# One graph-network kernel on one core: the message stage scales gathered rows instead of masks

## What is computed

```
xg0 = y0[edge_src]                                   # (E, 64)
xg1 = y1[edge_src]                                   # (E, 64, 3)
mid0 = w_a * xg0 * ea0
mid1 = w_b * einsum('euc,ec->eu', xg1, ea1) / sqrt(3)
mid2 = (w_c * xg0)[:, :, None] * ea1[:, None, :]
mid3 = (w_d * ea0)[:, :, None] * xg1
mids = concatenate([mid0, mid1, mid2, mid3])         # (E, 8 * 64)
agg  = segment_sum(mids, edge_dst, num_segments=n)   # (n, 512)
```

## Time and profile before

| what | value |
|---|---|
| median of three timed runs | 2001.14 us (1994.2 to 2003.65) |
| span of the profiled execution, first to last instruction | 2413.3 us |
| mean granted clock of TensorE | 0.875 of full speed |
| busy in the span: PE, PEld, DVE, ACT, POOL | 1891.3, 1517.9, 1125.8, 1021.4, 1104.5 us |
| DMA | 376.43 MB, mean 156 GB/s |

### The profile page before, as it was taken

The page is one execution under the profiler, slowest core; times in us unless marked ns, Lnnn a source line. Parts: engine busy times, 40 slices in busy tenths (PEclk is TensorE's granted clock), DMA queues, the critical chain, the costliest instruction groups (busy, mean ns, idle before and its releaser), DMA issues. The chain is left out here.

```text
span 2413.3 us, 38460 instructions
## 1 busy us (share of the span) xinstructions
PE 1891.3 (78%) x9911; PEld 1517.9 (63%) x9911; DVE 1125.8 (47%) x2791; ACT 1021.4 (42%) x3052; POOL 1104.5 (46%) x1499
## 2 busy tenths in 40 slices
PE   1368787877799858999455877787778789899699
PEld 1245454554466657999335766676767679777588
DVE  3532222222242374544664666565656669431322
ACT  2513343343353532333264555454545557454222
POOL 5547667666700004555375665565655550000243
PEclk7679999889999858999777888887888889999799
DMA  5636556565734026666544554555554553255553
GB/s 150 202 90 198 190 187 198 185 193 187 210 140 138 11 64 201 212 212 215 135 149 147 150 159 140 151 155 145 147 153 144 150 148 107 69 164 177 155 180 129
DMA packets 229197, 376.43 MB, mean 156 GB/s; under 512 B 66081, under 2 KB 114308, under 8 KB 228998
## 3 DMA queue, kind: packets, MB, share of 16 engines
q1 hardware_dynamic: 174820, 222.13, 31.0%
q0 software_dynamic: 52224, 150.15, 20.2%
q10 hardware_dynamic: 1954, 1.79, 0.2%
HBM read 275.38 MB, written 99.57 MB: 155 GB/s over the span
## 5 line engine op out<-in xcount | busy, mean ns | idle before, releaser
L1940 POOL DMA_INDIRECT msg_got<-y_dram,block_src x416 | 412.4, 991 | 293.5 <-DVE msg_prod L2012 139.7
L439 POOL DMA_INDIRECT ffn_w<-xn_dram,block_src x384 | 364.6, 949 | 219.2 <-issue 81.7
L1961 ACT ACTIVATE msg_scaled<-msg_plain,msg_w 128x125 f32<-128x125 f32 x1044 | 314.0, 386 | 280.1 <-DVE msg_plain L1993 234.6
L554 PE MATMUL sum_ps_bank<-ffn_w,sum_onehot 128*125 x928 | 270.5, 419 | 115.6 <-DVE sum_onehot L893 84.3
L554 PEld LDWEIGHTS sum_ps_bank<-ffn_w,sum_onehot 128*125 128x125 f32 x928 | 184.0, 206 | 264.6 <-issue 246.6
L881 DVE TENSOR_TENSOR agg<-sum_ps_bank,agg 125x256 f32 x232 | 98.4, 424 | 432.4 <-PE sum_ps_bank L554 216.5
L541 PE MATMUL sum_ps_bank<-sum_fc,sum_space 128*128 128x512 f32 x416 | 231.9, 644 | 68.9 <-ACT sum_space L639 48.3
L650 ACT ACTIVATE sum_space<-sum_ps_bank,sum_rec 128x128 f32<-128x128 f32 x416 | 131.0, 369 | 330.4 <-PE sum_ps_bank L541 159.5
L1982 PE MATMUL msg_ps_z<-msg_prod,msg_scaled 128*125 128x128 f32 x1416 | 207.5, 293 | 53.7 <-issue 53.0
L1982 PEld LDWEIGHTS msg_ps_z<-msg_prod,msg_scaled 128*125 128x125 f32 x1416 | 198.6, 206 | 72.4 <-issue 64.1
L2022 DVE TENSOR_TENSOR agg<-msg_ps_z,agg 125x512 f32 x232 | 159.4, 687 | 23.9 <-issue 5.2
(11 more groups left out here) (343 smaller groups left out, 3397.9 us busy)
## 6 DMA issues: line engine op xcount, KB each, us to landing
edge_w<-sum_space SPq DMA_DIRECT2D x52, 1040.0 KB
msg_w<-edge_w SPq DMA_DIRECT2D x174, 260.0 KB
ffn_run_w<-in_L_ffn_w SPq DMA_DIRECT2D x64, 512.0 KB
x_sb<-edge_w SPq DMA_DIRECT2D x58, 260.0 KB
ffn_rows<-agg SPq DMA_DIRECT2D x25, 448.0 KB
ffn_w<-in_L_ffn_w SPq DMA_DIRECT2D x16, 512.0 KB, 8.7
wd<-in_L_ffn_Wd SPq DMA_DIRECT2D x8, 1024.0 KB, 8.6
msg_got<-y_dram,block_src POOLq DMA_INDIRECT x416
```

The lines of the kernel that those rows point to most:

```text
L439: pool.indirect_dma_start(got[:, (b + 1) % RING, u, :], None, k.x if b < RAW else k.xn_dram, bass.IndirectOffsetOnAxis(ap=k.block_src[:, b ...
L554: last = pe.matmul(ps_sum[n % ZB][0:P, :], onehot[n % OB][:, u, :], got[:, ds(need % RING, 1), u, :].rearrange("p o d -> p (o d)"), start= ...
L1940: pool.indirect_dma_start(got[:, (b + 1) % RING, u, :, :].rearrange("p k v -> p (k v)"), None, k.y_dram, bass.IndirectOffsetOnAxis(ap=k.bl ...
L1961: last = act.activation(scaled[s % MB][:, x, c, :], plain[s % MB][:, c, :], ACT.Copy, scale=w[s % RS][:, c, D + x:D + x + 1])
```

## The change

ScalarE scales gathered rows instead of masks. For each column of 128 edges and each component x of the edge vector it multiplies two planes of the gathered row, plane 0 and plane x + 1, by that component, into a new buffer `turned` (two halves: plane 0 times each component, and plane x + 1 times component x). It reads the gathered rows by a register, and so waits for `blocks_in` and no longer for the mask. VectorE then forms all eight planes complete: it adds the three products of the second half to the dot product (two instructions, in a buffer `dots`), and multiplies planes 0 and 1 to 3 as before, planes 5 to 7 from the first half of `turned`, and plane 4 from `dots`. TensorE sums all eight planes under the plain mask, with one matmul of 512 columns for each column of edges. `scaled` is gone, `turned` has three buffers, and SyncE no longer waits for ScalarE.

```diff
@@ -1887,10 +1887,10 @@
 
         w = [borrow(CH * WREC).rearrange("p (c d) -> p c d", c=CH) if b == 1 else ph.sb(f"w{b}", [128, CH, WREC])
              for b in range(RS)]
-        plain = [borrow(CH * P).rearrange("p (c w) -> p c w", c=CH) if b == 1 else ph.sb(f"plain{b}", [128, CH, P])
-                 for b in range(MB)]
-        scaled = [borrow(3 * CH * P).rearrange("p (x c w) -> p x c w", x=3, c=CH) if b == 1 else ph.sb(f"scaled{b}", [128, 3, CH, P])
-                  for b in range(MB)]
+        plain = [ph.sb(f"plain{b}", [128, CH, P]) for b in range(MB)]
+        turned = [borrow(CH * 6 * MUL).rearrange("p (j c x v) -> p j c x v", j=2, c=CH, x=3) if b == 2
+                  else ph.sb(f"turned{b}", [128, 2, CH, 3, MUL]) for b in range(MB - 1)]
+        dots = [ph.sb(f"dots{b}", [128, CH, MUL]) for b in range(2)]
         prod = [borrow(CH * 8 * MUL).rearrange("p (c k v) -> p c k v", c=CH, k=8) if b == 2 else ph.sb(f"prod{b}", [128, CH, 8, MUL])
                 for b in range(XB)]
         ph.taken.append(k.x_put)
@@ -1898,8 +1898,8 @@
         ps_lanes, lanes_made, rest_zero = ph.ps("lanes", [128, P]), ph.sem("lanes_made"), ph.sem("rest_zero")
         w_in, got_in, blocks_in = ph.sems("w_in", RS), ph.sems("got_in", RING), ph.sem("blocks_in")
         rest, rested = ph.sb("rest", [128, 32]), ph.sem("rested")
-        masked, scaled_made, made, summed, added = (
-            ph.sem(x) for x in ("masked", "scaled_made", "made", "summed", "added"))
+        masked, scaled_made, made, summed, added, dotted = (
+            ph.sem(x) for x in ("masked", "scaled_made", "made", "summed", "added", "dotted"))
         block = ph.ctx.enter_context(nc.Block())
 
         @block.sync
@@ -1907,7 +1907,6 @@
             for s in range(NST):
                 if s >= RS:
                     sp.wait_ge(made, s - RS + 1)
-                    sp.wait_ge(scaled_made, s - RS + 1)
                 if s == 1:
                     sp.wait_ge(k.x_put, 32 * (NG - 1))
                 for h in range(2):
@@ -1951,36 +1950,45 @@
         def _(act):
             rest = k.agg[:, T // 2:T, :].rearrange("p t d -> p (t d)")
             act.activation(rest, k.ident[:, 0:1].to_broadcast([128, (T - T // 2) * 2 * D]), ACT.Copy, scale=0.0).then_inc(rest_zero, 1)
+
+            def place(n):
+                return act.value_load(k.pair_need[0:1, n:n + 1], min_val=1, max_val=NB)
+
+            need = [place(0), place(1)]
             for s in range(NST):
-                act.wait_ge(masked, s + 1)
+                if s == 1:
+                    act.wait_ge(k.x_put, 32 * (NG - 1))
                 act.wait_ge(w_in[s % RS], 32 * (s // RS + 1))
-                if s >= MB:
-                    act.wait_ge(summed, s - MB + 1)
-                for c in range(CH):
-                    for x in range(3):
-                        last = act.activation(scaled[s % MB][:, x, c, :], plain[s % MB][:, c, :], ACT.Copy,
-                                              scale=w[s % RS][:, c, D + x:D + x + 1])
+                act.wait_ge(blocks_in, need[1])
+                if s >= MB - 1:
+                    act.wait_ge(made, s - MB + 2)
+                following = []
+                for h in range(2):
+                    for u in range(KC):
+                        c = KC * h + u
+                        for x in range(3):
+                            last = act.activation(
+                                turned[s % (MB - 1)][:, :, c, x, :],
+                                got[:, ds(need[h] % RING, 1), u, 0:x + 2:x + 1, :].rearrange("p o k v -> p (o k) v"),
+                                ACT.Copy, scale=w[s % RS][:, c, D + x:D + x + 1])
+                    if s + 1 < NST:
+                        following.append(place(2 * s + 2 + h))
                 last.then_inc(scaled_made, 1)
+                need = following
 
         @block.tensor
         def _(pe):
             pe.matmul(ps_lanes[:, :], k.onesf[0:1, :], k.iota[0:1, 0:P], start=True, stop=True).then_inc(lanes_made, 1)
             for s in range(NST):
-                pe.wait_ge(scaled_made, s + 1)
+                pe.wait_ge(masked, s + 1)
                 pe.wait_ge(made, s + 1)
                 if s >= ZB // 2:
                     pe.wait_ge(added, 1 + 2 * (s - ZB // 2 + 1))
-                mask, by, p = plain[s % MB], scaled[s % MB], prod[s % XB]
+                mask, p = plain[s % MB], prod[s % XB]
                 for h in range(2):
-                    z = ps_z[(2 * s + h) % ZB]
                     for u in range(KC):
                         c = KC * h + u
-                        pe.matmul(z[0:P, 0:4, :], mask[:, c, :], p[:, c, 0:4, :], start=(u == 0), stop=False, skip_group_check=True)
-                    for x in range(3):
-                        for u in range(KC):
-                            c = KC * h + u
-                            last = pe.matmul(z[0:P, 4:6 + x:1 + x, :], by[:, x, c, :], p[:, c, 4 + x:8:3 - x, :],
-                                             start=False, stop=(x == 2 and u == KC - 1), skip_group_check=True)
+                        last = pe.matmul(ps_z[(2 * s + h) % ZB][0:P, :, :], mask[:, c, :], p[:, c, :, :], start=(u == 0), stop=(u == KC - 1))
                 last.then_inc(summed, 1)
 
         @block.vector
@@ -2000,18 +2008,25 @@
             def products(s, need):
                 p = prod[s % XB]
                 v = w[s % RS][:, :, 0:D].rearrange("p c (k v) -> p c k v", v=MUL)
+                from_0, from_1 = (turned[s % (MB - 1)][:, j, :, :, :] for j in range(2))
+                dot = dots[s % 2][:, :, :]
                 dve.wait_ge(w_in[s % RS], 32 * (s // RS + 1))
                 dve.wait_ge(blocks_in, need[1])
                 if s >= XB:
                     dve.wait_ge(summed, s - XB + 1)
+                dve.wait_ge(scaled_made, s + 1)
+                dve.tensor_tensor(dot, from_1[:, :, 0, :], from_1[:, :, 1, :], ALU.add).then_inc(dotted, 1)
                 for h in range(2):
                     y = got[:, ds(need[h] % RING, 1), :, :, :].rearrange("p o u k v -> p (o u) k v")
                     at = slice(KC * h, KC * h + KC)
-                    dve.tensor_tensor(p[:, at, 0:8:7, :], v[:, at, 0:4:3, :], y[:, :, 0:1, :].to_broadcast([128, KC, 2, MUL]), ALU.mult)
-                    for q in (1, 2):
-                        last = dve.tensor_tensor(p[:, at, 3 * q - 2:3 * q + 1, :], v[:, at, q:q + 1, :].to_broadcast([128, KC, 3, MUL]),
-                                                 y[:, :, 1:4, :], ALU.mult)
-                last.then_inc(made, 1)
+                    dve.tensor_tensor(p[:, at, 0, :], v[:, at, 0, :], y[:, :, 0, :], ALU.mult)
+                    dve.tensor_tensor(p[:, at, 1:4, :], v[:, at, 1:2, :].to_broadcast([128, KC, 3, MUL]), y[:, :, 1:4, :], ALU.mult)
+                    if h == 0:
+                        dve.wait_ge(dotted, 2 * s + 1)
+                        dve.tensor_tensor(dot, dot, from_1[:, :, 2, :], ALU.add).then_inc(dotted, 1)
+                dve.tensor_tensor(p[:, :, 5:8, :], v[:, :, 3:4, :].to_broadcast([128, CH, 3, MUL]), from_0[:, :, :, :], ALU.mult)
+                dve.wait_ge(dotted, 2 * s + 2)
+                dve.tensor_tensor(p[:, :, 4, :], v[:, :, 2, :], dot, ALU.mult).then_inc(made, 1)
 
             def add_sum(n, tile):
                 if n % 2 == 0:
```

## The result

The changed kernel takes 2106.98 us (median; 2103.58 to 2110.59), beside it the kernel before 1997.67: a ratio of 1.055, 95% interval 1.052 to 1.058, 109 us more. Forecast were 77 us more.

The account below looks back on a forecast made before the run. VectorE was taken to bound the message stage at 4.57 us a step, gathers and TensorE close behind; 0.66 us more a step over 116 steps, +77 us on 2001.14, gave 2078 us, range 2005 to 2118.

Parts of the forecast that it names:

- The accounting of the 412 us: Profiled execution's excess over the timed median: 262 us message stage, 111 us other gather stage, 39 us unassigned.
- the crawl: Stretches of the first profile where TensorE's or ScalarE's instructions come one at a time, 1.4 us apart; little in timed runs.
- VectorE sets the pace, +0.66 us a step: Message stage: VectorE's products grow from 2.54 to 3.20 us, the step to 5.23 us; 116 steps add 77 us.
- TensorE's saving is worth nothing: Message stage: TensorE needs 3.49 us a step, 0.87 less, which gives nothing back because VectorE is slower.
- The fall of the clock: Rival: TensorE, pausing each step, drops to 1.2 GHz and a 6.97 us step; up to 2280 us, chance 0.05.
- ScalarE hidden: Message stage: ScalarE's twelve scalings keep 3.6 us a step, and VectorE's wait for them is covered by some 4 us.
- Start and end cancel: Message stage: first scalings up to 3.6 us later at the start, about 3 us saved at the end.
- The two waits on 'dotted' look at an instruction with two others in between (0.66 us), longer than its 0.42 us: VectorE's waits on its own dot-product additions: covered by the two instructions in between.
- my last rival: VectorE's waits on its own results are bare, three of 0.22 us a step: another 77 us, 2155 us, chance 0.07.
- products without overlap: Upper end for VectorE's products: full durations count, 3.04 becomes 3.89 us a step, 99 us more instead of 77.
- Gathers already set the pace: Rival: message stage's gathers average 1.31 us, 545 us, so the change costs 62; gathers hiding it had chance 0.07.

Follow-up runs that it names:

- before_again: The kernel before the change, unedited, profiled once more: 1996.03 us.
- pe_full: Changed kernel with TensorE's old matmuls restored (two of 256 and six of 128 columns each half step): 2106.53 us, ratio 1.056.
- tiles_once: Changed kernel with two of VectorE's four register loads a step left out, so all sums go into the first rows: 2050.47 us, ratio 1.026.
- loads_more: Changed kernel with two more, unused register loads a step on VectorE: 2246.92 us, ratio 1.125.
- loads_mid: Changed kernel, VectorE reordered: products not needing the dot product, four register loads, second addition, first sum, plane 4, second sum, mask: 2080.09 us, ratio 1.043.
- breaks_after: Changed kernel, VectorE reordered so sums and mask break up the products and register loads precede the second addition: 2077.23 us, ratio 1.041.

## Why the prediction was right in kind and short in size

*The accounting of the 412 us* held: the crawl belonged to one execution.

*VectorE sets the pace, +0.66 us a step* held for the step: 3.21 us of products where 3.20 were worked out, and 128-element instructions 0.20 us apart. For the pace it held in the changed kernel; in the kernel before the gathers were the later by a little (before_again).

*TensorE's saving is worth nothing* held in pe_full. Its group takes 3.67 us, not 3.49, at a granted clock of 0.94 where pe_full has 1.00. The fall of the clock was a rival, with 2280 us: the clock did dip with pauses of 1.9 us in each step, but TensorE waits for VectorE all the same, 1.88 us a step.

*ScalarE hidden* held: 3.61 us for its twelve scalings, and VectorE waits for it twice in 1100 to 1680, 2.7 us together. *Start and end cancel* did not hold. The first product comes 5.65 us after the first mask, where before_again has 1.52: 4.1 us more. The end gave back not 3 us but 0.3: from the end of the last product to the start of the last sum are 6.85 us (1741.20 to 1748.05) instead of 7.19. TensorE is done there by 1746.45; VectorE's last three pairs of sums start 2.30 us apart, and 0.77 us of that is idle, in which VectorE finishes the two register loads of the next pair.

*The step that failed* is "The two waits on 'dotted' look at an instruction with two others in between (0.66 us), longer than its 0.42 us". The waits themselves are met in time. What I left out is what stands behind the second on VectorE: four register loads, three of which must be done before the first sum. They start only when that wait is met and cost 0.3 us a step. The same waits were in my last rival, as bare waits of 0.22 us each; tiles_once and loads_more show that it is the loads, not the waits' own length. The time came out inside the range, and that is partly luck: its upper part stood for products without overlap and for bare waits, and neither came.

The sum as measured: the first five steps of the stage cost 5 us more than before. In the other 110, 110 x 0.67 = 74 for the products, 110 x 0.31 = 34 for the pause, 28 x 0.36 = 10 for each fourth step, less 14 of waits for blocks that the slower step fills: 109, where 109 were measured. Forecast was the second of these terms.

*Gathers already set the pace* was nearer than its 0.07. They took the 1.31 us each that it named and ended the stage before the change, and the products' 74 us less the 14 of waits are its 62 but for 2 us. They did not hide the change, because the new step is longer than its four gathers. And with the pause taken out of the changed kernel (loads_mid, breaks_after) they are the bound again, and so of the 65 us that VectorE would give back only 27 and 30 come.

## What to carry to other kernels

Behind a wait on an engine's own result, look for register loads as well as for arithmetic: loads that nothing covers stand in no busy row, and the releaser that the profile names for the gap can be any engine. Ask the trace for the line that loads them, and to find their cost, add two and take two away. Where two engines are level, a shorter step on the one may be paid back by the other: measure the order as a whole before believing a hole that is filled.

## What was not expected of the hardware

The same gather usually takes 0.95 us, and up to 3.45 us when VectorE runs products with both inputs in SBUF; most such gathers end 0.9 us after VectorE's next product begins or after its first instruction with an input in PSUM. The Trainium skill, page "SBUF — State Buffer", section "🔬 SBUF: two separate sides", says that VectorE, with two SBUF inputs, and a GpSimd instruction that reads SBUF hold a shared pair of ports by an exclusive lock. The 1.70 us beside a product of 0.95 agree; for waits over several products in a row no run here shows why the lock isn't passed on at each boundary.

One execution of an unchanged program had a span of 2413.3 us where the next had 1994.3, with TensorE and ScalarE issuing every 1.2 to 1.4 us in places; nothing in the program explains it. And VectorE's delay of 0.36 us in every fourth step went away with two register loads fewer; its cause was not tried further and stays open.
